# A query projection of seven block products in place of eight, as a stage of its own between a feed-forward and the attention that uses it

## The reference, cut to what matters

```python
# third block: x is the residual stream after f0, ctx the context
h = layernorm(x)                                  # (2048, 1024)
q = (h @ wq)                                      # wq: (1024, 4096), 32 heads of 128
k = (ctx @ wk); v = (ctx @ wv)                    # 8 heads of 128
q = rope(q); k = rope(k)                          # rotary embedding over 256 positions
scores = einsum('bhgqd,bhkd->bhgqk', q, k) / sqrt(128)
w = softmax(where(mask, scores, -1e9))
x = x + tanh(g_xattn[1]) * (einsum('bhgqk,bhkd->bhgqd', w, v) @ wo)   # wo: (4096, 1024)
```

## Time and profile before

| what | value |
|---|---|
| median of three runs | 3116.79 us |
| the profiled execution, its own time | 3115.62 us |
| span of that execution in the trace | 3113.8 us |
| granted TensorE clock, mean | 0.996 |
| PE busy, share | 99% |
| f0, first to last of its product matmuls | 754 to 1028 us |
| attention units | 1028 to 2922 us |
| f1 products | 2922 to 3110 us |

### The profile page before, as it was taken

One profiled execution on the slowest core, in us unless ns is written; L12 is line 12 of the kernel. 1 busy time (PEld: TensorE's weight loads), 2 busy tenths in 40 slices (PEclk: granted clock), 3 DMA queues, 4 the chain that ended last, 5 costly groups with the idle time before them and its releaser, 6 DMA issues.

```text
span 3113.8 us, 40170 instructions
## 1 busy us (share of the span) xinstructions
PE 3072.3 (99%) x15136; PEld 2571.3 (83%) x15136; DVE 1949.3 (63%) x4650; ACT 1140.8 (37%) x2382; POOL 700.6 (22%) x576
## 2 busy tenths in 40 slices
PE   9999999999999899999999999999999999999999
PEld 7888778887778788888888888888888888888887
DVE  4333488887563777778666667666667666666432
ACT  4111466665222344445333334333333333333320
POOL 2422389885322133333000000000000000000231
PEclk9999999999999999999999999999999999999999
DMA  7332412114363567777655454455455454453621
GB/s 244 129 119 99 161 52 82 48 55 170 109 223 129 198 216 238 235 250 248 224 198 175 151 182 175 163 207 173 149 186 186 162 203 161 151 176 120 252 95 55
DMA packets 232861, 509.47 MB, mean 164 GB/s; under 512 B 23180, under 2 KB 58124, under 8 KB 232668
## 3 DMA queue, kind: packets, MB, share of 16 engines
q1 hardware_dynamic: 231948, 505.45, 47.5%
q10 hardware_dynamic: 720, 1.44, 0.1%
HBM read 364.23 MB, written 142.61 MB: 163 GB/s over the span
## 4 chain that ended last, share of the span: by engine, by line
PE 88%; DVE 4%; ACT 3%; POOL 3%; DMA 1%; issue 0%; SPq 0%; ACTq 0%
PE PB L150 27%; PE PB L151 27%; PE PB L152 27%; PE PB L2058 3%; PE PB L640 2%; POOL ac_paw L999 1%; POOL ac_cl L982 1%; ACT ac_w L723 0%; DVE ac_st L837 0%; PE PB L2464 0%; DMA wqd<-at_wql 0%; PE PB L1235 0%; ACT ac_w L764 0%; DMA at_rawo<-in_wo 0%; PE PB L2018 0%
## 5 line engine op out<-in xcount | busy, mean ns | idle before, releaser
L150 PE MATMUL PB<-at_woh,at_ah 128*128 128x512 f32 x1024 | 409.7, 400 | 1.8 <-ACT at_pth L2148 1.8
L2138 ACT ACTIVATE at_ss<-at_ss,at_sm,at_bs 128x256 f32<-128x256 f32 x512 | 301.7, 590 | 294.8 <-DVE at_sm L2244 294.8
L150 PE MATMUL PB<-at_hh,at_wqh 128*128 128x512 f32 x1024 | 401.1, 392 | 0.6 <-DVE at_hl L2185 0.6
L151 PE MATMUL PB<-at_hl,at_wqh 128*128 128x512 f32 x1024 | 400.6, 391 | 0.0
L152 PE MATMUL PB<-at_hh,at_wql 128*128 128x512 f32 x1024 | 399.5, 390 | 0.0
L151 PE MATMUL PB<-at_wol,at_ah 128*128 128x512 f32 x1024 | 399.2, 390 | 0.0
L152 PE MATMUL PB<-at_woh,at_al 128*128 128x512 f32 x1024 | 399.1, 390 | 0.0
L2222 DVE TENSOR_TENSOR at_t<-PB,at_rt 128x512 f32<-128x512 f32 x128 | 88.4, 691 | 434.2 <-PE PB L152 434.2
L2274 DVE SCALAR_TENSOR_TENSOR at_xt<-PB,gt,at_xt 128x512 f32<-128x512 f32 x256 | 190.7, 746 | 128.0 <-PE PB L152 127.9
L2155 ACT ACTIVATE at_ah<-PB 128x512 fp32r<-128x512 f32 x128 | 76.5, 598 | 472.0 <-PE PB L152 472.0
L152 PEld LDWEIGHTS PB<-at_hh,at_wql 128*128 128x128 f32 x1024 | 192.7, 188 | 41.2
(11 more groups left out here) (269 smaller groups left out, 7166.2 us busy)
## 6 DMA issues: line engine op xcount, KB each, us to landing
at_wqh<-wqd SPq DMA_DIRECT2D x96, 512.0 KB, 3.7
at_wql<-wqd SPq DMA_DIRECT2D x96, 512.0 KB, 4.5
at_woh<-wod SPq DMA_DIRECT2D x48, 1024.0 KB, 5.1
at_wol<-wod SPq DMA_DIRECT2D x48, 1024.0 KB, 7.5
at_rawq<-in_wq SPq DMA_DIRECT2D x32, 512.0 KB, 5.7
wqd<-at_wqh SPq DMA_DIRECT2D x32, 512.0 KB, 6.2
wqd<-at_wql SPq DMA_DIRECT2D x32, 512.0 KB, 7.3
at_rawo<-in_wo SPq DMA_DIRECT2D x32, 512.0 KB, 6.0
```

Of the source, the lines that this page charges most:

```text
L150: pe.matmul(o, ah, bh, start=start, stop=False)
L151: pe.matmul(o, ah, bl, start=False, stop=False)
L2138: m = act.activation(at_ss[:, s, c, :], at_ss[:, s, c, :], ACT.Exp, bias=z[:, 4 + c:5 + c], scale=at_bs[:, qn % 2, 8 + 2 * b + c % 2:9 + 2 ...
```

## The change

1. A stage `qp` stands between f0 and the attention. It computes all queries once and stores them rotated to HBM (`qd`); the attention only fetches (`fetch_q`) and splits them (`split_q`, low part on GpSimd). The stage works on 32 pairs: a pair of heads (16) by half of the tokens (two `sb`). For each pair the product is cut in 2 by 2 blocks, made of seven block products (12 matmuls of 512 columns each) with sums of weight blocks before and sums of results after. Before, the same output took eight: 128 projections of 24 matmuls are 3072, now 32 pairs of 84 are 2688.
2. The sums of weight blocks are made on GpSimd from the raw `wq`, which is fetched once for each `sb` and split anew; `wqd` is gone. The sums of token blocks come from f0's tail: after each tile is finished its rows are normalised (`stats2`, `norm2`, `rows2`), transposed (`turn` in f0) and combined (seven factors), and stored to HBM (`xod`), from which the stage fetches and splits them (`expand`).
3. In the stage VectorE sums the products, several of them from one PSUM bank into another, and rotates the result (`turn`, six operations for each half of a pair).
4. The attention's first steps and its units 0 to 5 are issued within the stage's last block (the last two pairs).
5. The attention's unit has a new order: `turn(u-2)`, `scores(u)`, first `output`, `weigh(u-1)`, `values(u-2)`, second `output`, then `split_wo(u)`; three weight tiles `at_ss` for two. `wo` parts are split one unit later than before in relation to `u`, and used in the unit after the second half's split.

```diff
         def f0_schedule(pair_begin, ...):
@@ f0_vector
+            def stats2(t):
+                s, xt = t % 2, f0_xt[t % NX]
+                on.wait_ge(*at("f0_dve", ("f", t, 1)))
...
+                for i in range(2):
+                    m = dve.bn_stats(f0_st2[:, s, 6 * i:6 * i + 6], xt[:, halves(i)])
...
+            def turn(t):
+                low, high = (BK[f0_turned(t, hf)].rearrange("p (c n) -> p c n", c=4) for hf in range(2))
...
+                dve.tensor_tensor(xo[3], low, xo[0], ALU.subtract).then_inc(*inc("f0_dve", ("xo", t, 3)))
...
@@ the stage
+        NP = H // 2
+        LASTP = 2 * NP - 1
+        NR = 7
+        Q_BLOCKS = [(0, 1)] + [(n,) for n in range(2, NP - 2)] + [(NP - 2, NP - 1), (NP, NP + 1)] + [(n,) for n in range(NP + 2, LASTP - 1)] + [
+            (LASTP - 1, LASTP)]
+        Q_ORDER = [(pair, i) for block in Q_BLOCKS for i in range(7) for pair in block]
+        def qp_bank(pair, i):
+            j = qp_at(pair, i)
+            return 5 + j % 3 if pair >= LASTP - 1 else (0, 1, 4, 5, 6, 7, 2, 3)[j % 8]
...
+            for block in Q_BLOCKS:
+                if block[0] in (NP + 2, LASTP - 2):
+                    yield
+                for i in range(7):
+                    for pair in block:
+                        do.product(pair, i)
+                        do.sum(pair, i)
+                        ahead = qp_at(pair, i) + NR - 1
+                        if ahead < len(Q_ORDER):
+                            do.prepare(*Q_ORDER[ahead])
...
+                    if i > 4:
+                        for pair in block:
+                            do.turn(pair, i - 5)
...
+                    if block[-1] == LASTP:
+                        yield
@@ GpSimd in the stage
+                if i == 0:
...
+                    pool.tensor_tensor(s1, a21, a22, ALU.add).then_inc(*inc("qp_pool", ("s", pair, 3)))
...
+                    pool.tensor_tensor(a21, a11, a21, ALU.subtract).then_inc(*inc("qp_pool", ("s", pair, 2)))
...
+                pool.tensor_tensor(qp_part(pair, i, 1), qp_weight(pair, i), asf(qp_part(pair, i, 0)), ALU.subtract).then_inc(
+                    *inc("qp_pool", ("w", pair, i)))
+                if i == 0:
...
+                    pool.tensor_tensor(a11, s1, a11, ALU.subtract).then_inc(*inc("qp_pool", ("s", pair, 1)))
...
+                if i == 4:
...
+                    pool.tensor_tensor(a12, a12, a11, ALU.subtract).then_inc(*inc("qp_pool", ("s", pair, 6)))
@@ the attention's schedule
-            for u in range(NU + 4):
+            for u in range(NU + 5):
...
+                if 2 <= u < NU + 2:
+                    do.turn(u - 2)
+                if u < NU:
+                    do.scores(u)
...
+                if u + 2 < NU:
+                    do.split_q(u + 2)
+                    if u + 4 < NU:
+                        do.fetch_q(u + 4)
+                m, k = (u - 5) // 4, (u - 5) % 4
+                if u > 4:
+                    do.output(m, 2 * k)
+                if 1 <= u < NU + 1:
+                    do.weigh(u - 1)
+                if 2 <= u < NU + 2:
+                    do.values(u - 2)
+                if u > 4:
+                    do.output(m, 2 * k + 1)
+                do.split_wo(u)
+                if u < 6 or u in (NU - 1, NU, NU + 1):
+                    yield
@@ at_half
-            n, k = u // 4, u % 4
+            n, k = (u - 1) // 4, (u - 1) % 4
             return (n, 0, k - 2) if k >= 2 else (n - 1, 1, k)
@@ weave
             for t in f0:
-                if t in (4, 6, -8, 8, "half", 10, 12, None):
-                    next(att)
+                if t in (10, 12, "begin", "odd", "rows", "turn"):
+                    next(qp)
+            for _ in range(2):
+                next(att)
+                next(qp)
+            next(att)
+            for _ in qp:
+                next(att)
```

More of the change, by code:

```diff
@@ L1308, in f0_tensor @@
             yield
-            yield from f0_schedule(lambda: None, first_chunk, first_end, begin, mid, odd, end)
+            yield from f0_schedule(lambda: None, first_chunk, first_end, begin, mid, odd, end, lambda: None, lambda: (turn(NT - 1, 0), turn(NT - 1, 1)))
         def f0_scalar(act, on):
@@ L1635, in f0_vector @@
             yield
-            yield from f0_schedule(first_begin, first_chunk, first_end, begin, mid, odd, end)
+            yield from f0_schedule(first_begin, first_chunk, first_end, begin, mid, odd, end, lambda: None, lambda: turn(NT - 1))
         def f0_gpsimd(pool, on):
@@ L1861, in none @@
                 pass
-            fetch_ahead = take = fetch_bias = fetch_x = bias = turn = flip = output = scores = stats = rows = norm = project = rest = none
-            weigh = values = split_wo = split_wq = load_wq = fetch_wq = keep_wq = fetch_rope = load_kv = none
+            fetch_ahead = take = fetch_bias = bias = turn = output = scores = none
+            weigh = values = split_wo = fetch_q = split_q = load_kv = none
         def at_schedule(do):
-            do.fetch_x(0, 0)
-            do.fetch_x(0, 1)
@@ L1934, in at_schedule @@
-                if new:
-                    do.turn(u - 1)
-                    do.output(n - 1, 2 * k)
-                if u < NU:
-                    do.scores(u)
-                if more and w in (29, 30):
-                    do.norm(qn + 1, w - 27)
-                ahead = u + 2 < NU and plain
-                if ahead:
-                    do.project(u + 2)
-                if u < 4:
-                    do.rest(u + 2)
-                    do.weigh(u)
-                if 2 <= u <= 4:
-                    do.values(u - 2)
@@ L1949, in at_schedule @@
-                if 1 <= u <= NU and plain and not new:
-                    do.turn(u - 1)
-                if more and w == 29:
-                    do.flip(qn + 1, 0, 0)
-                if ahead and u >= 4:
-                    do.rest(u + 2)
-                if n and not new:
-                    do.output(n - 1, 2 * k)
-                if not plain:
-                    do.weigh(u)
-                if more and w == 29:
-                    do.flip(qn + 1, 0, 1)
-                    do.fetch_x(qn + 1, 3)
```

801 lines of the change are left out of this document (477 added, 324 removed).

## The result

The changed kernel takes 3085.74 us (median of 4 runs, 3081.28 to 3088.74); the kernel before took 3115.51 us beside it (4 runs, 3111.69 to 3116.98). The ratio is 0.9905, 95% interval 0.9888 to 0.9922: faster by about 30 us. I had forecast 54.6 us less, 3061. The time lies inside the range (3026 to 3108), but nearly half of the gain forecast did not come. The profiled execution took 3088.74 us, its span 3086.9 (before 3115.62 and 3113.8), and the mean granted clock fell from 0.996 to 0.990.

The account below looks back on a forecast made before the run. TensorE, busy 99%, was taken to pace the attention except in its first units. 3115.6 - 87.5 - 15 + 5 + 0 + 17 + 0 + 26 = 3061 us, range 3026 to 3108, about 0.82.

Parts of the forecast that it names:

- Matmuls: Query projection on TensorE: an eighth fewer matmuls at 0.228 us each, -87.5 us; the rows' mean duration would say 150.
- The old beginning: Attention's first units: 12.2 us idle and half of 5.7 us at the lower clock both go, -15 us.
- f0 and the seam: f0's added work and the stage's start: a few half-microsecond waits, token-factor expansion nearly covered by four products, +5 us.
- The stage: Query stage in steady state: TensorE paces at 19.1 us a pair, VectorE, ScalarE and GpSimd fit within it, 0 us.
- Last block and hand-over: Stage's last two pairs with units 0 to 5: TensorE waits behind VectorE's rotations, 14 us plus 3 for clock, +17 us.
- The unit: Attention unit without projection: 9.13 us on TensorE, the VectorE and ScalarE loop of 8.1 us fits, 0 us.
- Splitting `wo`: First 32 attention units: raw fetch landing behind stores makes two units take 20.0 us for 18.26, 15 times, +26 us.
- The end: End of the attention: drains over five units in place of four, f1's tiles loaded earlier, 0 us.
- A: Rival for the whole kernel: TensorE paces everything, 3030 us, chance 0.18; landings of `at_rawo` under 6 us its sign.
- B: Rival in the attention: the unit's loop is longer than 9.13 us, at 9.6 us 3106 us, chance 0.12.
- C: Rival in the query stage: GpSimd paces it, deciding from 1.67 us an operation, 3161 us, chance 0.08.
- D: Rival: seam, last block and `wo` splitting at their upper bounds, two thirds of 12 + 13 + 30 more, 3095 us, chance 0.12.

Follow-up runs that it names:

- run 4: Changed kernel with the second of each pair's seven products computed twice, 384 matmuls more: 3163.37 us, ratio 1.0152 to the kernel before.
- Run 10: Changed kernel with f0's second statistics of a tile put behind the low parts of the next tile's factors: 3098.94 us, ratio 0.9942.
- run 6: Changed kernel with GpSimd's low part of the query weights made for only 1 of 64 columns from pair 5 on: 3076.07 us, ratio 0.9874.
- Run 1: Changed kernel with the four residual tiles fetched before the last rotations are stored: 3081.66 us, ratio 0.9890.
- run 9: Changed kernel with the attention's first units behind the stage's last block, none between its products: 3091.91 us, ratio 0.9922.
- Run 3: Changed kernel with the next raw slice of `wo` fetched ahead of the two 1 MB stores: 3069.02 us, ratio 0.9848.
- run 8: Changed kernel with residual tiles fetched early, last four rotations one behind each of four units, raw `wo` fetched before the stores: 3062.51 us, ratio 0.9826.
- runs 1 and 2: Run 1, and a second: changed kernel with the last two pairs' four rotations one behind each of four units, 3081.77 us, ratio 0.9892.

## Why the prediction was right, and where it was not

The sign and the range held; the sum was 25 us too low. Step by step:

*Matmuls, -87.5.* Right, and shown: the starts are 0.227 us apart in the stage, and run 4 moves the time by 77 us and not by 150, so the trap of the mean duration was one. What I did not see is that a part of this work had covered other engines: with it back, 7.7 us of waits in the stage are gone (run 4).

*The old beginning, -15.* Right: 12.2 us idle are gone, and with them 3 us of clock, half of the 5.7 us in which TensorE worked at the lower level.

*f0 and the seam, +5.* Measured about 11 (idle 10.4 less 2.3, and 3 of clock); the seam has 0.6 us. The direction and the mechanism stood in the text, the size was off: I took waits of half a microsecond, the trace has up to 1.8 us for `f0hl` and up to 2.4 for `f0xn`. Run 10 shows that f0 had less slack than I counted.

*The stage, 0.* Measured 8.6 us idle and about 3 of clock. The prices of all its operations were right but one. I had weighed the rule of the Trainium skill ("SBUF — State Buffer", section "SBUF: two separate sides"), by which a VectorE operation with two SBUF inputs and a GpSimd operation that reads SBUF exclude each other for a whole instruction, and let it hold GpSimd, which has slack. It held VectorE as well, in the very block where I had found VectorE 2 to 3 us over TensorE's time: the 14 expansions there took 26.5 us, where 14 of 1.21 are 17, and four of GpSimd's low parts among them took 7.9 us for 5.2. The trace agrees with the rule in run 6: with most of GpSimd's reading gone the same 14 took 18.7 us, and the kernel was 8 us faster. The step that failed here is the sentence that the rule changes no term, and it failed by reasoning and not by size.

*Last block and hand-over, +17.* Measured about 30 (22.8 idle, 7 of clock). The waits for `at_ptl` were right in kind: 8.9 and 4.1 us for the 8 and 6 predicted. The sentence that failed is that the residual rows come "in the same time": they came 11.36 us after VectorE had nothing else to do, since SP holds their fetch behind the stores of the last rotations, which wait for VectorE itself. TensorE waited 9.8 us for that. Run 1 shows that it was not alone: with this wait gone the hand-over's idle time fell by 6.1 us, and the raw slice behind the same stores still came late. And the lower clock was 7 us, not 3. Which share of that is a consequence of each wait the runs do not separate.

*Beginning early, inside the +17.* Worth 7 us at most, and not to be told from nothing (run 9).

*The unit, 0.* Right: 9.14 us for 9.13.

*Splitting `wo`, +26.* Right in mechanism, somewhat high in size: 12.8 us idle and 3 of clock, or nearly 20 us by the distance of the units, 1.4 a pair for the 1.75 taken. The landing behind the stores was taken rightly at 7.5 us in every second fetch: it was 6.7 to 9.5. TensorE's waits were eleven and not fifteen, and five of them were for `at_sm` and not for the low part. Run 3 let that fetch land 3 us sooner and the loss nearly ended, as the lower bound of the term said; it gave 17 us.

*The end, 0.* Idle 4.0 us and 2 of clock, a single wait for `at_ptl`: overlooked. The later units have 3.2 us of idle time; all of the attention behind its beginning had 2.9 before, so that is no loss.

Together -87.5 - 15 + 11 + 11.5 + 30 + 16 + 6 = -28, where the span fell by 26.9.

Of the rivals, A fell with the waits, though the 5.7 us in the middle of the landings, under its 6, was its sign: a median over both kinds of fetch could not tell. B fell with the 9.14 us, C with 1.36 us an operation. D came nearest (3095; two thirds of its 55 us are 37, which makes 3098): the hand-over at its upper bound, but `wo` below its own term, and the seam covered.

The result is thus a removal that gives 77 of its 87.5 us, beside additions that cost 47 us for the 33 expected. The time lies in the range because the range reached over rival D, and not because the sum was right: the hand-over and the stage cost 24 us more than their terms, f0 and the end 12 more, and only `wo` cost less. Of the losses, 23 us are a matter of order alone: run 8 took them back without one instruction less.

## What to carry to other kernels

Work taken from the pacing engine was also cover: before it is booked as gain, list what each other engine still has to do in that time, and its queues too. Where a wait is predicted, look what lands or ends within a few microseconds of it, since removing one wait of several close together gives less than its length (runs 1 and 2: some 4 us each for waits of 9). A fetch that is needed next goes ahead of large stores on the same queue; here this one exchange was worth 17 us, more than half as much as the whole change. And before a median is read, see whether it mixes two kinds of the same operation.

## What I had not expected of the hardware

- VectorE's rotation with both inputs in SBUF took 2.72 to 2.88 us beside a GpSimd subtraction of 2.7 to 2.9 us, and 0.69 alone; the same rotation with an input in PSUM took 0.68 to 0.70 us throughout the stage. Where a sum is kept decides not only its own price.
- Four VectorE scalings of one SBUF input took 2.22 us beside GpSimd's subtraction (1712.08 to 1714.43 us) for 1.14 alone, so operations with one tensor input can be held too. It was seen once, not tested.
- A mean granted clock of 0.990 for 0.996 looks like 18 us of 3087, of which TensorE lost about 15: in the hand-over the clock fell to its lower level in the waits and stayed there for some microseconds of work, and TensorE was idle for nearly half of that time too. The 22.8 us of waiting there cost 7 us more, about a third on top.
